# First ctx loaded in rows and turned by TensorE, batch 1's xn and probs turned by DMA, w2 loaded from GpSimd's queue

## The reference

```python
def _L0_xattn_ref(teacher_logits, teacher_features, Wq, bq, Wk, bk):
    query = jnp.einsum('bnc,dc->bnd', teacher_features, Wq) + bq
    key = jnp.einsum('bnc,dc->bnd', teacher_features, Wk) + bk
    energy = jnp.einsum('bnd,bmd->bnm', query, key)
    attention = jax.nn.softmax(energy, axis=-1)
    return jnp.einsum('bln,bmn->blm', teacher_logits, attention)

def _bit_quant(w):
    scale = jnp.maximum(jnp.mean(jnp.abs(w)), EPS)
    w_ternary = jnp.clip(jnp.round(w / scale), -1.0, 1.0)
    return w + jax.lax.stop_gradient(w_ternary - w)

def _L0_ffn_ref(x, w1, b1, w2, b2):
    w1q = _bit_quant(w1)
    w2q = _bit_quant(w2)
    h = jnp.einsum('bsd,fd->bsf', x, w1q) + b1
    h = jax.nn.gelu(h, approximate=False)
    return jnp.einsum('bsf,df->bsd', h, w2q) + b2

x = x + _L0_xattn_ref(_layernorm(x, axis=-1), ctx_1024, Wq, bq, Wk, bk)
x = x + _L0_ffn_ref(_layernorm(x, axis=-1), w1, b1, w2, b2)
```

## Time and profile before

| | us |
|---|---|
| median of 3 runs | 312.29 (311.95 to 313.38) |
| the profiled execution | 312.49 |
| its span | 310.7 |
| TensorE matmul busy | 303.9 (98%), 1401 instructions |
| VectorE busy | 153.7 (49%) |
| ScalarE busy | 143.9 (46%) |
| GpSimd busy | 109.2 (35%) |
| chain that ended last: TensorE | 96% |

### The profile page before, as it was taken

The page is one execution under the profiler, slowest core; times in us unless marked ns, Lnnn a source line. Parts: engine busy times, 40 slices in busy tenths (PEclk is TensorE's granted clock), DMA queues, the critical chain, the costliest instruction groups (busy, mean ns, idle before and its releaser), DMA issues.

```text
span 310.7 us, 3674 instructions
## 1 busy us (share of the span) xinstructions
PE 303.9 (98%) x1401; PEld 144.2 (46%) x1401; DVE 153.7 (49%) x295; ACT 143.9 (46%) x253; POOL 109.2 (35%) x111
## 2 busy tenths in 40 slices
PE   6799999999999999999999999999999999999996
PEld 3366544444444444444444444444444444444455
DVE  0888896764598853755308342445433003442101
ACT  2179998577723506542654604545440017762000
POOL 0276339999979960000903620000650000000000
PEclk9999999999999999999999999999999999999999
DMA  7899999674653992000032854000034100000011
GB/s 174 237 381 408 361 277 205 131 135 103 121 104 63 155 228 105 2 0 0 0 70 54 166 103 154 0 0 0 2 69 115 56 34 0 0 2 0 34 49 54
DMA packets 66706, 32.24 MB, mean 104 GB/s; under 512 B 59504, under 2 KB 60032, under 8 KB 66176
## 3 DMA queue, kind: packets, MB, share of 16 engines
q1 hardware_dynamic: 66368, 31.73, 40.4%
q10 hardware_dynamic: 320, 0.27, 0.4%
HBM read 15.21 MB, written 4.19 MB: 62 GB/s over the span
## 4 chain that ended last, share of the span: by engine, by line
PE 96%; DMA 2%; DVE 1%; SPq 0%; ACT 0%; issue 0%
PE ps_t L511 36%; PE ps_e L536 24%; PE ps_e L494 13%; PE ps_e L525 9%; PE ps_e L443 5%; PE ps_e L435 2%; PE ps_e L543 2%; PE ps_t L435 2%; DMA ctx_sb<-in_ctx 2%; PE ps_t L467 1%; PE ps_e L454 1%; PE ps_t L454 1%; SPq L247 0%; DVE ctxT L764 0%; ACT qkT L644 0%; DVE x_sb L1055 0%
## 5 line engine op out<-in xcount | busy, mean ns | idle before, releaser
L511 PE MATMUL ps_t<-x2T,w1T 128*128 128x512 f16 x512 | 112.1, 379 | 0.0
L706 ACT ACTIVATE ps_t<-ps_t,b_col 128x512 f32<-128x512 f32 x64 | 42.5, 665 | 96.6 <-PE ps_t L511 96.6
L511 PEld LDWEIGHTS ps_t<-x2T,w1T 128*128 128x128 f16 x512 | 50.1, 98 | 60.7 <-issue 0.6
L900 DVE SCALAR_TENSOR_TENSOR gT_lo<-ps_t,h_scale,gT_hi 128x512 f16<-128x512 f32 x64 | 45.1, 746 | 66.2 <-ACT gT_hi L711 66.2
L536 PE MATMUL ps_e<-w_raw,gT_hi 128*128 128x512 f16 x176 | 66.7, 379 | 0.0
L536 PE MATMUL ps_e<-w_raw,gT_lo 128*128 128x512 f16 x176 | 66.7, 379 | 0.0
L349 POOL TENSOR_TENSOR rstd<-var_eps,minus_half 128x4 f32<-128x4 f32 (+1 forms) x9 | 8.5, 947 | 99.7 <-DVE neg_mean L813 99.7
L711 ACT ACTIVATE gT_hi<-ps_t,h_scale 128x512 f16<-128x512 f32 x64 | 40.3, 684 | 0.0
L906 DVE SCALAR_TENSOR_TENSOR x_sb<-ps_e,h_unscale,x_sb 128x512 f32<-128x512 f32 x15 | 11.0, 748 | 57.9 <-PE ps_e L536 54.6
L536 PEld LDWEIGHTS ps_e<-w_raw,gT_lo 128*128 128x128 f16 x176 | 17.2, 98 | 21.4 <-issue 1.0
L536 PEld LDWEIGHTS ps_e<-w_raw,gT_hi 128*128 128x128 f16 x176 | 17.2, 98 | 21.1 <-issue 0.7
(11 more groups left out here) (86 smaller groups left out, 290.9 us busy)
## 6 DMA issues: line engine op xcount, KB each, us to landing
w_raw<-in_L_ffn_w SPq DMA_DIRECT2D x8, 1024.0 KB, 14.7
x_sb<-in_x SPq DMA_DIRECT2D x4, 1024.0 KB, 7.5
out<-x_sb SPq DMA_DIRECT2D x15, 256.0 KB, 2.6
ctx_sb<-in_ctx SPq DMA_DIRECT2D x16, 128.0 KB, 3.2
b_sb<-in_L_ffn_b SPq DMA_DIRECT2D x1, 256.0 KB, 7.2
w_raw<-w_raw SPq DMA_TRANSPOSE x16, 3.8
out<-x_sb SPq DMA_DIRECT2D x2, 128.0 KB, 1.7
x2n<-in_L_xattn_Wq ACTq DMA_DIRECT2D x1, 128.0 KB, 3.0
```

The costliest lines, as they stand in the source:

```text
L511: mm = nc.tensor.matmul(ps_t[t][:], w1T[:, k, j], x2T[:, b % 2, v, :, j], start=(v == 0 and j == 0), stop=(v == 1 and j == ND - 1))
L706: nc.scalar.activation(ps_t[t][:], ps_t[t][:], ACT.Gelu, scale=1.0 / LN_SCALE, bias=b1_col[:, k:k + 1]).then_inc(gelu_done, 1)
L900: nc.vector.scalar_tensor_tensor(out=gT_lo[:, k], in0=ps_t[t][:], scalar=h_scale[:, 0:1], in1=gT_hi[:, k], op0=ALU.mult, op1=ALU.subtract) ...
```

## The change

- ctx(0) comes in two DMAs with rows of 256 numbers. TensorE transposes it in eight 128x128 blocks into ps_t[0] and ps_t[1], VectorE copies it to ctxT. The first projection runs k = 0 for both halves, then k = 1, Wk first. copy_qk of batch 0 is cut in three, so that scores(0) can begin with the first tile of queries. The b1 transpose stands behind the projection, four warm-up matmuls go, total(B1) stands behind scores(0).
- xn and probs of batch 1 are turned by DMA like those of 2 and 3. turn_xn(1) and turn_probs(1) leave TensorE. Their stages lie in x2T[:, 1] and in gT_lo.
- TensorE's order becomes scores(1), attend(0), project(2), total(W1), scores(2), attend(1), hidden(0, 0), total(W2), hidden(0, 1) and so on. ScalarE's and VectorE's orders are changed with it.
- w2 is loaded by four DMAs from GpSimd's queue behind normalise_probs(1). SyncE's queue has the turns of batch 1 behind ctx(2), and b2, x(2), x(3) behind the w1 turns and ctx(3).

```diff
 QUANT_EPS = 1e-8
 WARM_UP = 10
-WARM_UP_2 = 4
 ROUND = 1.5 * 2.0 ** 23
 
 
@@ -40,6 +39,7 @@
     CH = WN // NCH
     GROUPS = NF // 4
     EARLY = 2
+    BY_PE = 1
     LAST = B - 1
...
@@ -64,6 +64,8 @@
         W_raw = x2n[:, 0:2, 0:C]
         W_columns = W_raw.rearrange("p s (i k) -> p s k i", k=NC)
         ctx_sb = sb("ctx_sb", [P, L // R, C // Q])
+        ctx0_rows = ctx_sb[:].rearrange("p a b -> p (a b)").rearrange("p (t c) -> p t c", t=NT)
+        ctx0_columns = ctx0_rows.rearrange("p t (i k) -> p t k i", k=NC)
         ctxT = sb("ctxT", [P, NC, L])
         qkT = sb("qkT", [P, 2, L])
...
+            if b < EARLY:
+                return x2T[:, 1].rearrange("p v h j t -> p v (h j t)")
             return w2_stage[:, 0]
 
         def probs_stage(b):
+            if b < EARLY:
+                return lo_stage[:, 1]
             return w2_stage[:, 1]
 
...
 
         @block.sync
         def _(sp):
+            def load_ctx0():
+                rows = ctx_in[0].rearrange("(t p) c -> p t c", p=P)
+                for h in range(2):
+                    sp.dma_start(ctx0_rows[:, 2 * h:2 * h + 2], rows[:, 2 * h:2 * h + 2]).then_inc(ctx0_here[h], 16)
+
             def load_ctx(b):
-                if b:
-                    sp.wait_ge(ctxT_ready, b)
+                sp.wait_ge(ctxT_ready, b)
                 for q in range(Q):
                     sp.dma_start(ctx_sb[q * R:(q + 1) * R], ctx_view[b, q]).then_inc(ctx_here, 16)
 
             def load_x(b):
...
             def turn_xn(b):
                 if b > EARLY:
                     sp.wait_ge(attn_ready, NT * b)
-                sp.wait_ge(xn_hi_done, NT * (b - EARLY + 1))
-                turn(xnT(b), xn_stage(b), 0, xnT_here[b - EARLY])
-                sp.wait_ge(xn_lo_done, NT * (b - EARLY + 1))
-                turn(xnT(b), xn_stage(b), 1, xnT_here[b - EARLY])
+                sp.wait_ge(xn_hi_done, NT * (b - BY_PE + 1))
+                turn(xnT(b), xn_stage(b), 0, xnT_here[b - BY_PE])
+                sp.wait_ge(xn_lo_done, NT * (b - BY_PE + 1))
+                turn(xnT(b), xn_stage(b), 1, xnT_here[b - BY_PE])
 
             def turn_probs(b):
-                sp.wait_ge(probs_hi_done, NT * (b - EARLY + 1))
-                turn(probsT(b), probs_stage(b), 0, probsT_here[b - EARLY])
-                sp.wait_ge(probs_lo_done, NT * (b - EARLY + 1))
-                turn(probsT(b), probs_stage(b), 1, probsT_here[b - EARLY])
+                sp.wait_ge(probs_hi_done, NT * (b - BY_PE + 1))
+                turn(probsT(b), probs_stage(b), 0, probsT_here[b - BY_PE])
...
-            load_ctx(0)
-            load_x(0)
+            load_ctx0()
             sp.dma_start(bqk[:, 0:1], bq.rearrange("(p a) -> p a", a=1)).then_inc(bqk_here, 16)
             sp.dma_start(bqk[:, 1:2], bk.rearrange("(p a) -> p a", a=1)).then_inc(bqk_here, 16)
+            load_x(0)
             load_ctx(1)
             load_x(1)
-            load_w(0, 0)
-            load_w(0, 1)
-            load_w(1, 0)
-            load_w(1, 1)
+            load_w1(0)
+            load_w1(1)
             load_ctx(2)
-            sp.dma_start(b2_sb[:], b2.rearrange("(a d) -> a d", a=1).to_broadcast([P, D])).then_inc(b2_here, 16)
-            load_x(2)
-            load_x(3)
+            turn_xn(1)
+            turn_probs(1)
             turn_first_x2(0)
             turn_w1(0)
             turn_first_x2(1)
             for c in range(1, NCH):
                 turn_w1(c)
             load_ctx(3)
+            sp.dma_start(b2_sb[:], b2.rearrange("(a d) -> a d", a=1).to_broadcast([P, D])).then_inc(b2_here, 16)
+            load_x(2)
+            load_x(3)
             for c in range(NCH):
                 turn_w2(c)
...
                     nc.gpsimd.tensor_scalar(chunk_whole(m, c), src, -ROUND, 1.0, ALU.add,
                                             ALU.mult).then_inc(rounded, 1)
 
+            def load_w2():
+                for j in range(ND):
+                    pool.dma_start(w2_raw[:, j], w_views[1][:, j]).then_inc(w_here[1][j // 2], 16)
+
             nc.gpsimd.memset(ident[:], 0.0).then_inc(ident_zero, 1)
             pool.wait_ge(ident_zero, 1)
             nc.gpsimd.affine_select(out=ident[:], in_=ident[:], compare_op=ALU.not_equal, fill=1.0, base=0,
@@ -405,6 +421,7 @@
             normalise_probs(0)
             layernorm(1)
             normalise_probs(1)
+            load_w2()
             layernorm2(0, range(0, 2), 0)
             layernorm2(0, range(2, NT), 1)
...
         @block.tensor
         def _(pe):
-            def warm_up(times):
-                for _ in range(times):
-                    nc.tensor.matmul(ps_e[0][:], gT_lo[:, 0, 0:P], gT_lo[:, 0], start=True, stop=True)
+            def first_projection():
+
+                for h in range(2):
+                    pe.wait_ge(ctx0_here[h], 16)
+                    for k in range(NC):
+                        for t in (2 * h, 2 * h + 1):
+                            mm = nc.tensor.transpose(ps_t[k][:, t * P:(t + 1) * P], ctx0_columns[:, t, k], ident[:])
+                        if h == 1:
+                            mm.then_inc(ctx0T_ready, 1)
+                pe.wait_ge(WT_done, 1)
+                pe.wait_ge(ctx0T_done, 1)
+                for s in (1, 0):
+                    nc.tensor.matmul(qk_bank(0, s)[:], WT[:, s, 0], ctxT[:, 0], start=True, stop=False)
+                pe.wait_ge(ctxT_ready, 1)
+                for s in (1, 0):
+                    nc.tensor.matmul(qk_bank(0, s)[:], WT[:, s, 1], ctxT[:, 1], start=False,
+                                     stop=True).then_inc(qk_ready, 1)
 
             def project(b, free):
...
             def scores(b, tiles, free):
-                pe.wait_ge(qkT_done, 2 * b + 2)
+                pe.wait_ge(qkT_done, 2 * b + 3 if b else 2)
                 for t in tiles:
                     free(t)
...
                         if k == 0:
-                            pe.wait_ge(exp_done, NT * EARLY + t + 1)
+                            pe.wait_ge(x2_done, NT + t + 1)
+                            if t == 3:
+                                pe.wait_ge(total_read, W2 + 1)
                         for part in (gT_hi, gT_lo):
                             mm = nc.tensor.matmul(y_bank(0, t)[:], part[:, k, t * P:(t + 1) * P], w2T[:, k],
...
             pe.wait_ge(b1_here, 16)
             nc.tensor.transpose(ps_e[3][:, 0:NF], b1_rows[:], ident[0:NF, 0:NF]).then_inc(b1T_ready, 1)
-            warm_up(WARM_UP_2)
-            pe.wait_ge(WT_done, 1)
-            project(0, lambda s: None)
-
-            total(B1, ps_t[3])
 
             def free(t):
-                if t == 3:
+                if t == 1:
+                    pe.wait_ge(qkT_done, 3)
+                elif t == 3:
                     pe.wait_ge(b1_col_done, 1)
             scores(0, range(NT), free)
+            total(B1, ps_t[3])
             project(1, lambda k: None)
             turn_xn(0)
             turn_probs(0)
             scores(1, range(NT), lambda t: pe.wait_ge(xn0_read, t + 1))
-            turn_xn(1)
-            attend(0, lambda t: pe.wait_ge(exp_done, NT + t + 1), [0, 1])
-            turn_probs(1)
-            attend(0, lambda t: pe.wait_ge(exp_done, NT + t + 1), [2, 3])
-            pe.wait_ge(bank_read[3], N_PROBS1 + 1)
+            attend(0, lambda t: pe.wait_ge(exp_done, NT + t + 1), range(NT))
+            project(2, lambda s: pe.wait_ge(bank_read[s], N_PROBS0 + 1))
+            pe.wait_ge(bank_read[3], N_PROBS0 + 1)
             total(W1, ps_t[3])
-            attend(1, lambda t: pe.wait_ge(x2_done, t + 1), range(3))
-            project(2, lambda s: pe.wait_ge(bank_read[s], N_PROBS1 + 1))
-            attend(1, lambda t: pe.wait_ge(x2_done, t + 1), [3])
-            pe.wait_ge(total_read, W1 + 1)
-            total(W2, ps_t[3])
-            scores(2, range(NT), lambda t: pe.wait_ge(x2_done, NT + t + 1))
+            scores(2, range(NT), lambda t: pe.wait_ge(x2_done, t + 1))
+            attend(1, lambda t: pe.wait_ge(exp_done, NT * EARLY + t + 1), range(NT))
 
             def scores_free(b):
                 def free(t):
@@ -600,7 +620,10 @@
                         pe.wait_ge(x2_done, NT * b + t - 1)
                 return free
 
-            for g in range(GROUPS):
+            hidden(0, 0)
+            pe.wait_ge(x2_done, 2 * NT)
+            total(W2, ps_e[3])
+            for g in range(1, GROUPS):
                 hidden(0, g)
...
 
         @block.scalar
         def _(act):
+            def copy_first_qk():
+
+                for s, columns, n in ((1, slice(0, L), 1), (0, slice(0, P), 2), (0, slice(P, L), 2)):
+                    act.wait_ge(qk_ready, n)
+                    nc.scalar.activation(qkT[:, s, columns], qk_bank(0, s)[:, columns], ACT.Identity,
+                                         bias=bqk[:, s:s + 1]).then_inc(qkT_done, 1)
+
             def copy_qk(b):
                 for s in range(2):
...
             act.wait_ge(bqk_here, 16 * 2)
-            copy_qk(0)
```

(51 more changed lines are left out.)

86 lines of the change are left out of this document (43 added, 43 removed).

## The result

| | before | after |
|---|---|---|
| median, run side by side | 312.84 us (311.95 to 313.77, 4 runs) | 319.85 us (318.91 to 320.19, 4 runs) |
| the profiled execution, its span | 312.49, 310.7 us | 320.19, 318.4 us |
| start of hidden(0, 0) | 59.16 us | 66.76 us |
| TensorE, matmul busy | 303.9 us (98%), 1401 instructions | 303.1 us (95%), 1373 instructions |
| share of the chain that ended last: TensorE | 96% | 85% |

The ratio is 1.0227, with a 95% interval of 1.0196 to 1.0258: the kernel is 2.3% slower. The forecast was 316.2 us with a range of 313.2 to 319.6. The sign was right, the time lies 0.25 above the range. Ratios and their intervals leave out executions that are over 1.5% above the fastest of the same kernel; of all that follow this touches only one kernel, named there.

The account below looks back on a forecast made before the run. TensorE bounds the kernel, with 96% of the chain of waits. Its terms moved hidden(0, 0) from 59.16 to 63.0; with 0.14 for total(W2), less 0.1, that is +3.9 on 312.29: 316.2 us, range 313.2 to 319.6.

Parts of the forecast that it names:

- first maximum of batch 1: On VectorE, forecast to start at 27.75 us instead of 26.89, ahead of the exp that attend(0) waits for.
- turn_probs(1) gone: Removing this turn from inside attend(0) on TensorE, where nothing waits, was to save 1.75 us.
- wait for total(W1): TensorE was to idle behind project(2) until copy_qk(2) and two sums of w1 were done: +3.5 us, bounds 3.2 and 4.0.
- rounding of w1 starts: GpSimd was to start rounding w1 at 49.6 us, not 46.41, since total(W1) comes later.
- wait for the turns: attend(1) was to wait for batch 1's DMA turns, queued beside w2's load: +2.4 us, bounds 0 and 5.8.
- The start and where its gain goes: scores(0) was to start 2.3 us earlier, the gain lost on VectorE before attend(0): worth -0.1 us.
- The floor from GpSimd's rounding: Later rounding of w1 was to hold hidden(0, 0) to 61.45 us at the earliest: at least +2.3 us.
- rival 1: Batch 1's DMA turns don't suffer and the floor from GpSimd's rounding decides: +2.4, 314.7 us, chance 0.26.
- the overlap of 1.2: Batch 1's turns and w2's load were assumed to overlap by 1.2, putting the last landing at 52.5 us.
- rival 2: Batch 1's turns starve behind w2, hidden(0, 0) comes 5.8 us after 60.6: +7.3, 319.6 us, chance 0.18.
- rival 3: TensorE's clock falls to 1.2 GHz after idle stretches, scores(2) costing 3.5 us more: about 318 to 320, chance 0.06.

Follow-up runs that it names:

- first-part run: The kernel before with only ctx(0) in rows, first_projection, copy_first_qk and total(B1) behind scores(0): 313.56 us, ratio 1.0045.
- the run in which the turns didn't suffer: Changed kernel, sums 6 and 7 of w1 ahead of copy_qk(2), w2 loaded in two pairs, ahead of normalise_probs(1) and behind layernorm2(0): 315.05 us, ratio 1.0099.
- the three runs with 12.9 to 13.0: Changed kernel with w2 issued behind layernorm2(0) (319.55 us); w2 on SyncE's queue (322.33 us); w2 in two pairs, sums first (315.05 us).
- the version that won: Kernel before with ctx(0) turned by TensorE, b1 transpose ahead of the first projection, scale_gelu behind batch 0's second inverse: 311.52 us, ratio 0.9974.

## Why the prediction was right and wrong

| step | forecast | measured |
|---|---|---|
| start of the first projection | 7.35 | 7.35 |
| start of scores(0) | 11.4 | 11.48 |
| first maximum of batch 1 | 27.75 | 27.81 |
| attend(0) | 29.3 | 29.35 |
| turn_probs(1) gone | -1.75 | attend(0) takes 10.37 in one piece |
| wait for total(W1) | +3.5 | +3.45 (46.60 - 39.72 - 3.43) |
| rounding of w1 starts | 49.6 | 49.87 |
| wait for the turns | +2.4 (0 to 5.8) | +4.4 (54.71 - 50.3) |
| clock of attend(1) | 0 | +1.7 |
| path over low_x2 and x2's second turns | not priced | not before 63.5, an estimate |
| hidden(0, 0) | 63.0 | 66.76 |

**The start and where its gain goes**: right, and for the reason given. The b1 transpose behind the projection puts moments(0) at 11.72 and the rest follows on VectorE. The first-part run shows it by itself. What the forecast didn't name is that taking this limit away shows two more in a row, total(B1) and then the sums; only with all three settled is the gain of 0.8 there.

**The wait for total(W1)**: right to 0.05 us, and by its chain: the second half of project(2), copy_qk at 43.35, two sums, the total. Putting the sums first cut it to 0.65.

**The floor from GpSimd's rounding**, rival 1: it was never reached, since hidden(0, 0) came at 66.76, behind the 61.45 that it stood for. No run here tests its size. Rival 1's 314.7 is near the 315.05 of the run in which the turns didn't suffer, but by luck: what held that run was the path over low_x2.

**The wait for the turns**: the term that was mis-sized. The last landing came at 54.6; the forecast had 52.5 and the upper bound 55.9. attend(1) waited 4.4 and not 2.4. The failed step is the overlap of 1.2, taken from the start of the kernel, where a share of 1.20 stood for 1 us. Over 33.40 to 44.00 the share was 0.91 and over 44.00 to 49.60 it was 1.15, and over all of 33.0 to 54.9 the two queues add up to 53.2% + 47.4%, just over 1.00. Adding up w2's 10.4 us and the turns' 10 was nearly right; rival 2 had said so, from rows in which the share of either kind alone was already 1.00 or more. The rule that the forecast quoted from the Trainium skill ("DMA: Bandwidth & Descriptors", section SWDGE vs HWDGE vs iDMA), that issuers meet in the same 16 engines and go packet by packet, agrees with the first turn's 14.3 us beside w2's rows of 8 KB. Read as I read it, shorter rows should share more evenly. The run with rows of 2 KB does not bear that out, both became slower, but it changed more than the packets.

**The clock**, rival 3: the second step that failed, a term put at nothing. Right in kind, wrong in place and weight: the forecast gave it a chance of 0.06 and priced it on scores(2) at half speed throughout. It fell after the second idle stretch, on attend(1), for 1.7. In four other runs with the same 3.28 of idle it fell on scores(2): their record is 5.24 us long with w2 behind the turns, 5.38 with b1 early and with w2 on SyncE's queue, 6.57 with w2 in rows of 2 KB, against 3.68. What decides between them these runs don't show. The rule that the forecast quoted from the Trainium skill ("TensorE: Matmul & The Clock Gate", section Part 1: The HAM clock gate), that an idle engine falls back to the lower level, agrees with these four and with the second stretch of the changed kernel, and not with its first.

**A path that the forecast left out.** It took each feeder's slack from the kernel before, where low_x2 stood ahead of the maxima of batch 2. In the new order the second pair of x2's turns hangs on the fourth maximum, 13.0 us ahead of hidden(0, 0). By that path even the forecast's 63.0, and more so rival 1's 61.45, could not have been reached: 63.5, an estimate from 50.53 and the three runs with 12.9 to 13.0. It didn't set the time of the changed kernel, where TensorE came to hidden(0, 0) later than that; the second pair hung on attend(1)'s first tile there, and the first weight load of hidden(0, 0) still waited 0.3 us for it.

**The rivals were not exclusive.** Upper-end turns and a fallen clock came together, 2.0 and 1.7 above the forecast, and the second came of the first: the late turns made the idle time ahead of attend(1), and the clock fell behind it. Their sum is the 3.7 by which the forecast was short. A range whose top is one rival's result leaves out the two at once. Rival 2's 319.6 is near the measured time by luck: it had 5.8 for the turns alone, which measured 4.4.

## What to carry to other kernels

A bulk load placed "where the queues are free" must be priced against the DMA transposes that follow on another queue: add up the engine time of both, allow no overlap, and put the whole amount ahead of the last of them. When an order is changed, follow the path to every transfer that the next stage needs, here x2's second pair: a wait that ends with a DMA says nothing of who made it late, so look at whether the transfer was slow or issued late. When an early gain is lost, find each limit on the feeding engine one after another before judging the edit; here two misses stood ahead of the version that won. And filling or removing one idle stretch helps only up to the next feeder's deadline, so look at what is late next for every such step, the clock's share too.
